# Graph attention on 32 graphs: normalized rows split in SBUF and turned by DMA, and another order of the last slot

## The reference

```python
h = jnp.maximum(_layernorm(x, axis=-1), 0.0)          # x: (32, 256, 512)
q, k, v = split_heads(h @ Wq.T), split_heads(h @ Wk.T), split_heads(h @ Wv.T)   # 16 heads of 32
a = jnp.einsum('bhnd,bhmd->bhnm', q, k) * 512 ** (-0.5) + (adj + adj)[:, None]
row_nonzero = jnp.any(a != 0, axis=-1, keepdims=True)
a = jnp.where(row_nonzero, a, -jnp.inf)
p = jax.nn.softmax(a, axis=-1)
p = jnp.where(jnp.isnan(p), 0.0, p)
o = jnp.einsum('bhnm,bhmd->bhnd', p, v).transpose(0, 2, 1, 3).reshape(32, 256, 512)
return x + o @ Wo.T
```

## Time and profile before

| What | us |
|---|---|
| median of 3 runs | 1005.82 (1004.63 to 1005.83) |
| the profiled execution | 1005.16 |
| its span, first to last instruction | 1003.4 |
| PE busy | 959.6 |
| ACT busy | 934.5 |
| POOL busy | 862.3 |
| DVE busy | 850.0 |
| mean granted clock of PE | 0.989 of full |

### The profile page before, as it was taken

One profiled execution on the slowest core, in us unless ns is written; L12 is line 12 of the kernel. 1 busy time (PEld: TensorE's weight loads), 2 busy tenths in 40 slices (PEclk: granted clock), 3 DMA queues, 4 the chain that ended last, 5 costly groups with the idle time before them and its releaser, 6 DMA issues.

```text
span 1003.4 us, 33752 instructions
## 1 busy us (share of the span) xinstructions
PE 959.6 (96%) x11580; PEld 660.2 (66%) x11580; DVE 850.0 (85%) x3092; ACT 934.5 (93%) x3049; POOL 862.3 (86%) x936
## 2 busy tenths in 40 slices
PE   5879999999999999999999999999999999999965
PEld 4656776666677666777666677766666776667632
DVE  6778998888989888898988889988889898888863
ACT  5799999999999999999999999999999999999992
POOL 2278998989998898999888899989889988889894
PEclk9989999999999999999999999999999999999979
DMA  6289999999999999999999999999999999999995
GB/s 251 49 148 195 183 190 194 183 193 186 190 191 184 195 178 187 194 199 180 192 177 198 183 203 184 189 194 178 198 183 197 186 191 193 177 185 176 175 175 119
DMA packets 573818, 183.62 MB, mean 183 GB/s; under 512 B 547024, under 2 KB 555216, under 8 KB 573648
## 3 DMA queue, kind: packets, MB, share of 16 engines
q1 hardware_dynamic: 573648, 181.48, 100.9%
HBM read 29.36 MB, written 16.78 MB: 46 GB/s over the span
## 4 chain that ended last, share of the span: by engine, by line
PE 56%; DVE 28%; issue 8%; ACT 5%; POOL 1%; DMA 1%; DVEq 0%; POOLq 0%; ACTq 0%; SPq 0%
PE ps L1045 35%; DVE logits L752 15%; PE ps L1113 9%; PE ps L1063 7%; DVE stats L649 4%; ACT probs L547 3%; PE ps L942 3%; DVE q_lo L815 2%; DVE o_norm L782 2%; PE ps L1089 1%; DVE some L770 1%; ACT p L560 1%; PE ps L1019 1%; DMA w_nat<-in_L_gnn_Wq 1%; DVE row_min L752 1%
## 5 line engine op out<-in xcount | busy, mean ns | idle before, releaser
L430 POOL TENSOR_TENSOR p<-probs,p 128x512 f16<-128x512 f32 x512 | 586.4, 1161 | 89.9 <-ACT p L560 89.7
L547 ACT ACTIVATE probs<-logits,row_min 128x256 f32<-128x256 f32 x1024 | 513.6, 511 | 3.8 <-DVE row_min L752 3.8
L752 DVE CUSTOM_DVE_ANT_0 logits<-ps,adj_s,sigma 128x256 f32<-128x256 f32 x1024 | 438.0, 475 | 7.1 <-PE ps L1063 7.0
L560 ACT ACTIVATE p<-probs 128x512 f16<-128x512 f32 x512 | 323.5, 632 | 0.0
L1045 PE MATMUL ps<-ht_hi,w_hi 128*128 128x256 f16 x1024 | 280.2, 274 | 7.7 <-DVE q_lo L815 2.6
L1045 PE MATMUL ps<-ht_lo,w_hi 128*128 128x256 f16 x1024 | 279.4, 273 | 0.0
L1045 PE MATMUL ps<-ht_hi,w_lo 128*128 128x256 f16 x1024 | 279.4, 273 | 0.0
L547 ACT ACTIVATION_READ_ACCUMULATOR probs<-logits,row_min 128x1 f32 x1024 | 209.8, 205 | 0.0
L1045 PE MATMUL ps<-wo,o_hi 128*128 128x512 f16 x496 | 149.2, 383 | 3.8 <-POOL o_lo L456 3.8
L1045 PEld LDWEIGHTS ps<-ht_hi,w_hi 128*128 128x128 f16 x1024 | 100.1, 98 | 36.1 <-DVE q_lo L815 13.0
L1045 PEld LDWEIGHTS ps<-ht_lo,w_hi 128*128 128x128 f16 x1024 | 100.4, 98 | 14.0
(11 more groups left out here) (90 smaller groups left out, 1571.0 us busy)
## 6 DMA issues: line engine op xcount, KB each, us to landing
xs<-in_x SPq DMA_DIRECT2D x32, 512.0 KB, 4.6
out<-xs SPq DMA_DIRECT2D x64, 256.0 KB, 2.9
adj_raw<-in_adj SPq DMA_DIRECT2D x32, 256.0 KB, 3.2
pt<-p SPq DMA_TRANSPOSE x256, 4.0
w_nat<-p SPq DMA_TRANSPOSE x256, 3.4
w_nat<-in_L_gnn_Wq SPq DMA_DIRECT2D x2, 512.0 KB, 5.4
w_nat<-in_L_gnn_Wk SPq DMA_DIRECT2D x1, 1024.0 KB, 8.3
w_nat<-in_L_gnn_Wv SPq DMA_DIRECT2D x1, 1024.0 KB, 11.3
```

The costliest lines, as they stand in the source:

```text
L430: g.tensor_tensor(p16[:, c % 2, k, 1], probs[:, h % 4].rearrange("p u n -> p (u n)"), p16[:, c % 2, k, 0], ALU.subtract).then_inc(p_split, 1)
L547: e = a.activation(probs[:, h % 4, u, :], logits[:, h % 4, u, :], ACT.Exp, bias=row_min[:, t.par(d), u, h:h + 1], scale=-1.0, accum_out=ro ...
L560: a.activation(p16[:, c % 2, k, 0], probs[:, h % 4].rearrange("p u n -> p (u n)"), ACT.Copy)\
L752: v.tensor_tensor_reduce(out=logits[:, h % 4, u, :], in0=ps[:, S_BANK + h % HC, N * u:N * u + N], in1=adj_s[:, t.par(d), u, :], scale=sigm ...
```

## The change

It has two parts.

Batches 3 to 31 (`h_by_dma`, 29 slots): PE no longer turns xn, and nothing goes through AUX_BANK for it. The Relu and the split are made of xn in SBUF, in rows: `round_h` on ACT (u = 0, step 5) and `rest_of_h` on DVE: for u = 0 at step 6 one subtraction, for u = 1 at step 10 a max with 0 into the hi half, a wait for it, and the subtraction. The parts lie in h16, a part of the weights' space that is free by then. At step 11 SP issues one DMA transpose of both blocks and both parts (16 blocks of 128x128) into ht, which now holds ht_hi and ht_lo in the order block, part and chunk; a projection's moving operand of 256 columns is now two pieces of 128. DVE's ln_mean_var gets a wait for the earlier xn; POOL's layer norm waits for h_split in place of the turns; PE's q01 waits for the transpose.

The last slot and the tail: the scores of the last four heads go ahead of o0. These four heads are not rounded, split or turned by DMA: PE turns the fp32 probabilities into the score banks (steps 12 to 15), DVE (heads 0, 1 of the group) and ACT (2, 3) round, and DVE subtracts for all four. In the tail o_hi is made by ACT and o_lo by DVE in place of POOL. `project_last` does two chunks per call, block by block, at steps 0 and 5.

```diff
-        ht_hi = sb("ht_hi", [P, 2, NC, N], F16)
-        ht_lo = sb("ht_lo", [P, 2, NC, N], F16)
+        ht = sb("ht", [P, 2, NU, 2 * NC, P], F16)
+H_TURNED = 3
+H_BY_ACT = (0,)
+H_HI_STEPS, H_LO_STEPS = (5, 5), (6, 10)
...
+        def by_pe(b, h):
+
+            return b == NB - 1 and h >= H - HC
...
+                    if s == 11 and later(t, 2) and h_by_dma(t.batch(2)):
+                        b = t.batch(2)
+                        sp.wait_ge(h_split, NU * (b - H_TURNED + 1))
+
+                        sp.wait_ge(pj_full, NJ * t.batch(0) + 6)
+                        sp.dma_start_transpose(ht[:, b % 2].rearrange("p u l n -> p (u l) n"),
+                                               h16[:, 0:NU].rearrange("p u n -> p (u n)")).then_inc(ht_in, 16)
...
-                if d == 2:
-
-                    pool.wait_ge(aux_full, aux_after("h", t.batch(1), 1))
+                if h_by_dma(b - 1):
+
+                    pool.wait_ge(h_split, NU * (b - H_TURNED))
...
-                    if s == 7 and t.prev:
+                    if s == 7 and t.prev and t is not tail:
                         take_o(t, -1, 1)
...
+            def round_h(b, u):
+
+                act.wait_ge(xn_ready, NU * b + u + 1)
+                h_rows_free(act, b)
+                a.activation(h16[:, u, 0:D], xn[:, u, :], ACT.Relu).then_inc(h_hi_act, 1)
...
+            def rest_of_h(b, u):
+
+                n = b - H_TURNED
+                if u in H_BY_ACT:
+                    dve.wait_ge(h_hi_act, len(H_BY_ACT) * n + H_BY_ACT.index(u) + 1)
+                else:
+                    dve.wait_ge(xn_ready, NU * b + u + 1)
+                    h_rows_free(dve, b)
+                    v.tensor_scalar(h16[:, u, 0:D], xn[:, u, :], 0.0, None, ALU.max).then_inc(h_hi_dve, 1)
+                    dve.wait_ge(h_hi_dve, (NU - len(H_BY_ACT)) * n + u - len(H_BY_ACT) + 1)
+                v.scalar_tensor_tensor(out=h16[:, u, D:2 * D], in0=xn[:, u, :], scalar=0.0,
+                                       in1=h16[:, u, 0:D], op0=ALU.max, op1=ALU.subtract).then_inc(h_split, 1)
...
+                    if t is last and s >= 12:
+                        if s < 14:
+                            round_last(s - 12)
+                        rest_last(s - 12)
+                    if t is tail and s == 6:
+                        rest_last_o()
...
+                    if t is last and s == 8:
+                        scores(t, 3)
                     for j, half in halves(t, s):
                         if t.uses(j):
                             project(t, j, half)
...
+                    if t is last and s >= 12:
+                        turn_last_probs(s - 12)
+                    if t is tail and s in (0, 5):
+                        project_last(s // 5)
```

More of the change, by code:

```diff
@@ L93, in emit @@
         w16 = w_nat.bitcast(F16)
+        h16 = w16[:, 2]
         w_max = sb("w_max", [P, 4])
@@ L173, in emit @@
         ln_stats = sem("ln_stats")
+        h_hi_act = sem("h_hi_act")
+        h_hi_dve = sem("h_hi_dve")
+        h_split = sem("h_split")
+        ht_in = sem("ht_in")
         rstd_ready = sem("rstd_ready")
@@ L230, in emit @@
             for at, key in sorted(slot_uses):
+                if key[0] == "h" and h_by_dma(key[1]):
+                    continue
                 if 0 <= key[1] < NB and not (key[0] == "y" and key[2] not in Y_C):
@@ L304, in h_turns, with h_parts, h_rows_free @@
             at = (10, 13) if t.first else (5, 8)
-            return [k for k in range(2) if at[k] == s and later(t, 2)]
+            return [k for k in range(2) if at[k] == s and later(t, 2) and not h_by_dma(t.batch(2))]
         def h_rests(t, s):
             at = (10, 13) if t.first else (6, 10)
-            return [k for k in range(2) if at[k] == s and later(t, 2)]
+            return [k for k in range(2) if at[k] == s and later(t, 2) and not h_by_dma(t.batch(2))]
+        def h_parts(t, s, steps):
+            return [u for u in range(NU) if steps[u] == s and later(t, 2) and h_by_dma(t.batch(2))]
+        def h_rows_free(eng, b):
+            if b == H_TURNED:
+                eng.wait_ge(wo16_in, 16 * NC)
+            else:
+                eng.wait_ge(ht_in, 16 * (b - H_TURNED))
         first = Slot(0, -1, False, False, True)
@@ L561, in round_probs, with round_last, round_last_o @@
                  .then_inc(p_hi, 1)
+            def round_last(j):
+                act.wait_ge(last_turned, j + 1)
+                a.activation(pt(NC - 1, j)[:, 0:2 * NU, :], ps[:, S_BANK + j, :].rearrange("p (l n) -> p l n", l=2 * NU),
+                             ACT.Copy).then_inc(last_hi_act, 1)
+            def round_last_o():
+                act.wait_ge(o_ready, 2 * NB)
+                a.activation(o_hi[:, (NB - 1) % 2, 2:4, :], o_norm[:], ACT.Copy).then_inc(last_o_hi, 1)
             def take_q(t, g):
@@ L628, in slot @@
                     round_probs(t, s + 1)
+                    if t is last and s in (14, 15):
+                        round_last(s - 12)
+                    if t is tail and s == 6:
+                        round_last_o()
                     for k in h_turns(t, s):
                         take_h(t.batch(2), k)
+                    for u in h_parts(t, s, H_HI_STEPS):
+                        if u in H_BY_ACT:
+                            round_h(t.batch(2), u)
             run(act, slot)
@@ L862, in slot @@
                             take_h(t.batch(2), k)
+                        for u in h_parts(t, s, H_LO_STEPS):
+                            rest_of_h(t.batch(2), u)
                     for b, u in residuals(t, s):
@@ L982, in _ @@
             W = (w_hi, w_lo)
-            HT = (ht_hi, ht_lo)
             O = (o_hi, o_lo)
@@ L1028, in project @@
                     need(pe, pj_taken[j % 2], bank_free_at(t, j))
-                    if j == 0:
+                    if j == 0 and h_by_dma(t.batch(1)):
+                        pe.wait_ge(ht_in, 16 * (t.batch(1) - H_TURNED + 1))
+                    elif j == 0:
                         pe.wait_ge(aux_taken, aux_after("h", t.batch(1), 1))
@@ L1080, in turn_probs, with turn_last_probs @@
                 m.then_inc(aux_full, 1)
+            def turn_last_probs(j):
+                pe.wait_ge(logits_ready, NU * H * NB)
+                pe.wait_ge(probs_ready, H * NB - HC + j + 1)
+                for u in range(NU):
+                    for mh in range(NU):
+                        m = tr(ps[:, S_BANK + j, P * (2 * u + mh):P * (2 * u + mh) + P],
+                               probs[:, j, u, P * mh:P * mh + P], ident[:])
+                m.then_inc(last_turned, 1)
             def turn_norm(t, d, p):
@@ L1105, in values @@
                 for c in (2 * p, 2 * p + 1):
-                    for k in range(HC):
-                        pe.wait_ge(pt16_in[c][k], 16 * (t.batch(d) + 1))
+                    if by_pe(t.batch(d), HC * c):
+                        pe.wait_ge(last_split, HC)
+                    else:
+                        for k in range(HC):
+                            pe.wait_ge(pt16_in[c][k], 16 * (t.batch(d) + 1))
                     for mh in range(NU):
@@ L1163, in slot @@
                         turn_norm(t, 0, 0)
-                    if s % 4 == 0:
+                    if s % 4 == 0 and not (t is last and s == 8):
                         scores(t, s // 4 + 1)
```

83 lines of the change are left out of this document (57 added, 26 removed).

## The result

| | before | after |
|---|---|---|
| median of 4 runs | 1005.23 us | 1041.82 us (1040.7 to 1042.84) |
| ratio, 95% interval | | 1.0364 (1.0346 to 1.0382) |
| profiled execution; span | 1005.16; 1003.4 us | 1040.7; 1038.9 us |
| mean granted clock | 0.989 | 0.990 |
| one slot, mean | 29.50 us | 30.76 us |

The account below looks back on a forecast made before the run. It took a loop closed along PE, 29.22 us of the 29.51 period, as the bound; the change makes it 30.0, so 1005.2 + 14.5 - 4.5 = 1015.2 us. Own range 1007 to 1024, with rivals 984 to 1046.

Parts of the forecast that it names:

- The removals: In 29 slots: PE's first four turns of xn -0.50 us, DVE's waits for ACT -0.17 and -0.16; loop 29.22 to 28.39.
- The additions at step 10: On DVE, ht_lo (-0.61 us) becomes a max (+0.34), a wait for its result (+0.12) and a subtraction (+0.68); loop 28.92.
- the new wait: At step 10 max and subtraction wait for POOL's p splits, 0.1 and 1.0 us, together 1.1 (bounds 0 and 2.2); loop 30.0.
- From 510.55 PE works without a gap ... and stands 0.29: PE from output projection to second norm turn's end: 14.25 us without a gap, then 0.29 slack; loop 29.22.
- The last slot: Reordered scores, earlier o_lo, and o_hi and o_lo off POOL were to save 4.5 us at the end, bounds 2 and 7.
- if the end gains nothing, the six DVE operations took it: Sign for the last slot: six of the eight added PSUM copies and subtractions, some 0.6 us each, fall on DVE.
- (2): Rival at step 10: two whole waits, 2.2 us, period 31.1, 1047 us; chance 15%.
- (1): Rival at step 10: subtraction slips in before POOL's next split, price nothing; 983 us with no wait; chance 20% with half ways.
- (3): Rival at step 10: max holds no second port, costs 0.6 us; subtraction waits some 0.4; loop 29.6, 1003 us; chance 10%.
- (4): Rival: extra transposes fill the DMA queue, p^T lands late for the values; 1.5 us a slot gives 1044 us; chance 4%.
- (5): Rival: PE's turns were the only bound and all 0.93 us a slot goes off; 974 us; chance 6%.
- The clock: Granted clock falls, to 0.83 from 960 to 970, only in the thin last slot.

Follow-up runs that it names:

- e4: Kernel before plus a max, a wait for it and a subtraction on eight columns on DVE at step 10 of 30 slots: 1058.05 us.
- e21: Kernel before with neg_mean and var_s made by POOL instead of DVE, xn keeping its operands and addition: 995.5 us.
- e17: e3 with the DMA transpose of the rows cut from sixteen blocks to one, all waits kept: 1029.54 us.
- e24: e17 with some and some_qk as reciprocals and neg_mean and var_s made by POOL: 993.81 us.
- e10: Kernel after with DVE's some, some_qk and neg_mean replaced by reciprocals, its new operations kept: 1031.22 us.
- e20: e1 with one line more: in the last slot DVE takes o_norm at step 12 instead of step 14: 1003.47 us.
- e1: Only the last slot of the change; xn turned by PE in all batches as in the kernel before: 1006.52 us.
- e16: Kernel after with the DMA transpose of the rows cut from sixteen blocks to one, all waits kept: 1041.1 us.
- e13: Kernel before plus one DMA transpose of that size per slot, from a constant tensor to a spare one: 1025.49 us.
- e3: Kernel after with DVE's three new operations replaced by maxima along the row, leaving out the split of the rows: 1031.63 us.
- e8: e3 with DVE's some, some_qk and neg_mean replaced by reciprocals: 1027.47 us.
- e7: Kernel after with ACT rounding both halves of the rows and DVE taking the second rest at step 8: 1033.16 us.
- e12: e7 with the DMA transpose of the rows at SP's step 9 instead of 11: 1025.35 us.
- e9: Kernel before with DVE's some, some_qk and neg_mean replaced by reciprocals, nothing else: 1002.36 us.

## Why the prediction was wrong

**The removals**: right. The first piece fell by 0.48 us for the 0.50 forecast.

**The additions at step 10 and the new wait**: right in sum, and the split of the wait wrong. The steps -0.17, -0.16, -0.61, +0.34, +0.12, +0.68 and +1.1 sum to +1.30 for the second piece; it rose by 1.27. The max was put at 0.42 us without a wait. Its shortest of 29 was 0.77, the median 1.18, and it waited every time, so its own length must be worked out: a subtraction of 0.69 that waits ends 0.55 behind POOL's split, so 0.14 of it is over by then; the max ends 0.28 behind, which makes it 0.42, an estimate. The Trainium skill's VectorE: DVE Perf Modes, section on the perf-mode tiers, has such an operation at two elements a cycle. The runs agree in that it needs about half of the subtraction's time behind POOL. The formula in that page's section on the TRN2 errata, which the prediction used, gives 0.33, an estimate; the same section of the Trainium skill says that it comes out short, and here it does, against 0.42. (With 0.33 as the length the sum would have been 0.09 less, not 0.02.) With 0.42 the max waits 0.76 in 24 slots and 0.35 in five, and the subtraction waits 0.84 (1.53 less 0.69) in every other slot: together 1.1 us a slot, as forecast. The 0.1 and 1.0 that I had put it together from came as 0.7 and 0.4 in the mean, so that the sum fits is in part luck. That DVE and POOL shut each other out for a whole instruction is as e4 shows it (0.93 us for eight columns); SBUF — State Buffer of the Trainium skill, section on the two separate sides, has that rule, and the runs agree.

**The failed step** is "From 510.55 PE works without a gap ... and stands 0.29". I took the loop home along PE, which has 0.29 us of slack there, and put everything new against a loop of 29.22. The way home without slack is another, over ACT and DVE. Two rows of DVE's timeline in the kernel before show it:

```profile
513.25 0.69 DVE L805 SCALAR_TENSOR_TENSOR v_lo<-ps,v_hi 128x512 f16<-128x512 f32 x1 [1.25 <-ACT v_hi L587]
...
515.68 0.74 DVE L843 SCALAR_TENSOR_TENSOR xs<-ps,out_scale,xs 128x512 f32<-128x512 f32 x1
```

The second v_lo waits for ACT, which works without a gap up to that v_hi. From 513.25 on DVE works through o_norm, both residuals, the statistics, neg_mean and var_s to the end of q_lo at 525.03, with 0.2 us of idle time in all; the residual comes straight behind o_norm and waits for nothing of PE's. The loop of the kernel before is therefore 29.50 from the start, and e21 shows it: 0.70 us off DVE's part of that way and nothing off PE's, and the slot comes down to 29.25, next to the 29.22 that I had read as PE's way, with PE's wait for q_lo gone. This alone is 0.29 x 29 = 8 us of the 27 missing. The 13.0 us of waits for q_lo that I had quoted was the row that said so: where PE waits in each of 30 slots, PE's way has slack, however small the wait is.

**The step that was not there** is the rest of the fourth piece, the 0.45 us that the third and fourth rose by, 13 us in 29 slots. I priced waits where the change adds operations and took the old small operations (some, some_qk, neg_mean) at their old lengths. The change moved DVE against POOL, and their waits changed: in e17, where the new operations wait for nothing and the blocks are gone, they are 1.05 us a slot longer than in the kernel before, and the kernel is 25 us slower; with them gone (e24) it is 11 us faster. Taking them out of the changed kernel does not give the 13 us back one for one: in e10 they are gone and the new operations wait longer, so 10.6 us came off where 34 were forecast. In the changed kernel itself the phase differs from slot to slot, hence 29.83 and 31.68 in turn.

**The last slot**: -4.5 us forecast (bounds 2 to 7), nothing came. I had written that "if the end gains nothing, the six DVE operations took it". e20 shows that what counted was not their length but their place, o_norm behind them, and behind o_norm POOL, PE's projection and the last norm. With o_norm ahead of them the end gains 3 us more than in e1, which is 1.5 us under the kernel before by the medians: a third of the term came, and the rest of it stays open.

The three together, 8 + 13 + 4.5 = 26, are all but one of the 27 us between 1015.2 and 1041.8. The two right steps say the same: forecast -0.50 + 1.30, measured -0.48 + 1.27, so 0.80 a slot; I had booked 0.5 of it, the rest having been hidden in a slack that was none.

**The rivals.** (2), two whole waits at step 10, had 1047 for nearly the right time and the wrong reason: the waits of the second piece are 1.1 us a slot and not 2.2, although in every other slot there are two of them. (1), no wait, is out: the max waits in all 29 slots. (3), a max with no second port, is out: it is held in every slot. (4), the DMA queue, was dismissed with "p transposes land in 4.0 us without a growing queue" and costed at nothing. For the changed kernel nothing is right (e16), but for a wrong reason: the median landing says little about the few that are late, and the same blocks cost 20.6 us where slots are 29.50 long (e13). (5), PE's turns as the only bound, is out.

**The clock.** The prediction has it fall only in the thin last slot; the page of the kernel before shows 0.8 of full in the third of 40 slices too. It has no part in the loss: the mean is 0.989 before and 0.990 after.

**Left open.** Why e3 and e17 settle into that phase and not another, and which part of the change moved them there: the phase comes out of the whole loop of DVE, ACT and POOL, and I could not forecast it. Further, what the change would be worth with all port operations out of the fourth piece and the full sixteen blocks: the nearest run is e8, with 1027.5 us, sixteen blocks, no waits of port operations and no split, where PE waits for the turned rows.

## What to carry to other kernels

Where an engine waits in every turn, even 0.4 us, the loop closes through what it waits for and not through its own work; check the way without slack against the period to the last hundredth before adding anything to another. When two engines shut each other out, the price is not in the instruction but in the moment: moving, shortening or removing work elsewhere re-deals the waits of all operations of that form, so count all of them in the loop and get the cheap ones off the lock first (here two operations of two columns, moved to the other engine, gave 9 us). And a resource for which nothing waits yet, here the DMA queue, can be the next bound as soon as what hides it is mended (e7, e8, e12).

## What the runs showed that I had not expected

- A wait for POOL can be handed on: with neg_mean made a reciprocal (0.17 us), var_s behind it went from 0.16 to 0.74 us (e9); with the same edit in e8 and e10 it did not. Reciprocals and maxima along a row showed no such wait in any slot; TENSOR_SCALAR on two SBUF columns did, up to 1.13 us in the kernel after.
- POOL's TENSOR_SCALAR on 128x512 with the mean out of an interleaved tensor and a subtraction: 2.08 us in all 64 instances, against 0.77 with its own tensor and an addition.
- One more DMA transpose of 2048 columns in each slot, read by nobody: +20.6 us (e13), with its data landing in 5.7 us at the median and p's median going only from 4.0 to 4.1.
- Two operations of eight columns on DVE a slot: +53 us (e4).
